# Macaron block on one core: four heads' scores on one wait, and features of the second feed-forward's first three groups made during attention

## The chip, the cores and the metric

The kernel runs on one NeuronCore of a Trainium2 chip. Five engines run their own streams of instructions and meet only at semaphores: PE (TensorE, matrix products into PSUM), ACT (ScalarE, exp, GELU and copies), DVE (VectorE, elementwise work, sums, 32x32 transposes), POOL (GpSimd) and SP (issues the DMAs). PSUM has eight banks of 128 x 512 float32. The metric is the device time of one execution in microseconds (us), the median of the runs.

## The reference, cut to what matters

```python
# x: 2 x 1024 x 128 float32; 8 heads of 8; 8 experts of 128 -> 256 -> 128; all inputs float32
def ffn(x):                                 # x already layer-normed, no affine part
    logits = x @ gate_w.T + gate_b          # 8 experts
    logits = logits * rsqrt(mean(logits**2) + eps) * rms_w
    g, idx = top_1(softmax(logits / 0.5))
    norm_g = masked(g) / (masked(g) + 1e-6)
    h = gelu(einsum('nd,edh->neh', x, w1) + b1)     # every expert, every token
    y = einsum('neh,ehd->ned', h, w2) + b2
    return (y * norm_g[:, None, None]).sum(axis=1)
def attn(x):
    q, k, v = heads((layernorm(x) * ln_w + ln_b) @ w_qkv)
    q, k = l2norm(q), l2norm(k)
    return merge(softmax(causal(8.0 * q @ k.T)) @ v) @ w_out
x = x + 0.5 * ffn(layernorm(x))
x = x + attn(layernorm(x))               # attn normalises once more
x = x + 0.5 * ffn(layernorm(x))
```

(`masked` keeps the gate of the chosen expert.)

## The kernel before, in words

The 2048 tokens are four groups of 512. Everything lives in SBUF between the first load and the last store. There are three stages: the first feed-forward (about 119 us), attention (about 119 to 188 us) and the second feed-forward (186 to 287 us).

**Feed-forward.** The eight experts' 2048 hidden units are 16 chunks of 128. For each group and chunk, PE makes three products up (`up`, L455 on) and three down (`down`, L479 on): float32 operands are held as a rounded part (`_hi`) and a remainder (`_lo`), so one product is hi*hi + hi*lo + lo*hi, each 128 x 512. ACT applies GELU from PSUM, DVE makes the remainder `h_lo`, and a ring of four PSUM banks and four SBUF slots keeps them apart. A group also needs its features: layer statistics and normalisation on DVE (`stats`, `aggregate`, `normalise`), a reciprocal root on POOL (`ln_once`), four transposes on PE (`ln_transpose`, L431), two copies on ACT (`ffn_features`, L727: the features `xf`, and their rounded part `xT_hi`), and the remainder `xT_lo` on POOL (`low_features`, L348). In each feed-forward the features of group g+1 are made while group g runs, at the chunks that `AT` names. In the second feed-forward only those of group 0 are made earlier, in attention.

**Attention.** Heads are packed four at a time (a "quad") with the operands of each head on its own 32 rows of the PE array. The list `steps` holds 80 half steps s; step k is the two half steps 2k and 2k+1, that is, four heads of one quad over one tile of 128 keys and up to 512 queries (`item`). A half step's scores (`scores`, L592 on) fill two PSUM banks, a set. There are three sets (`S_SETS`), six banks. ACT takes the exp of a whole set in one instruction (`exp_scores`, L797), 1024 elements a partition, or 512 where the last item of a causal block has half the queries; it writes `probs`. POOL masks the diagonal. PE then makes probabilities times values (`pv`, L606) three steps later (`PV_LAG`). PE's order in step k is: scores 2k, scores 2k+1, `pv(k-3)`, and at some steps a job. Before half step s is written, PE waits for the exp that read its set, s-3 (`set_reader`). So scores 2k wait for exp 2k-3, and scores 2k+1 for exp 2k-2.

**Jobs.** The list `jobs` (L242) is side work put between the products: PE's `fill(n)` (L631) writes one PSUM bank, DVE's `empty(n)` (L1137) takes it away, and every fill waits until the job before is emptied. A job with step number j is filled right after `pv(j)`, in PE's loop at k = j+3. With q1, q2, q3 = 6, 20, 26, the jobs are the last group's q, k and v; the output projections `project` of each pair of quads, which need `output` on DVE (L1118: a transpose of the accumulated output, reciprocal, scaling, transpose); and `ffn_ln` (L1159), the transposes of the normalised group 0 for the second feed-forward, at q3+5 = 31. All DVE work of attention stands in one list in the order of the jobs (L1196 on).

Of the kernel before, what the change touches and what calls it, by code (L numbers as in the profile page):

```python
# [30 lines left out]
P = 128  # L31
# [3 lines left out]
GROUP_TILES = 4  # L35
# [63 lines left out]
def build(nc, x, ln_w, ln_b, w_qkv, w_out, gate_w, gate_b, rms_w, w1, b1, w2, b2, out):  # L99
# [9 lines left out]
    with ctx:  # L109
# [118 lines left out]
        for st in steps:  # L228
# [16 lines left out]
                (q2 + 4, "project", (1, 0)), (q2 + 5, "project", (1, 1)),  # L245
                (q3 + 1, "project", (2, 0)), (q3 + 2, "project", (2, 1)), (q3 + 5, "ffn_ln", 0),
# [22 lines left out]

        def v_part(quad):  # L270
            return slice(SPREAD * quad, SPREAD * quad + HEAD_DIM)
# [13 lines left out]
        def ffn_groups(eng, layer, group):  # L285


            group(0)
            if layer == 0:
                for g in range(1, GROUPS - 1):  # L290
                    group(g)
            else:
                with eng.Fori(1, GROUPS - 1) as g:
                    group(g)
            group(GROUPS - 1)


# [50 lines left out]
        def low_features(eng, g):  # L348
            part = ds(g * GROUP, GROUP)
            eng.tensor_tensor(xT_lo[:, part], xf[:, FFN, :], xT_hi[:, part].bitcast(f32), ALU.subtract).then_inc(xT_ready, 1)  # L350
# [79 lines left out]
        def _(pe):  # L430
# [16 lines left out]
            def gate_product(F):  # L447
                pe.wait_ge(xf_done[FFN], F + 1)
                pe.wait_ge(gate_logits_done, F)
                for i in range(GROUP_TILES):  # L450
                    m = pe.matmul(ps[:, BANK_GATE, EXPERTS * i:EXPERTS * i + EXPERTS], xf[:, FFN, P * i:P * i + P],  # L451
                                  cols[:, COL_GATE:COL_GATE + EXPERTS], start=True, stop=True)
                m.then_inc(gate_mm, 1)

            def up(layer, F, c, g):  # L455
# [8 lines left out]
                if c == 0:  # L464
                    if layer == 1 and isinstance(g, int) and g == 0:
                        pe.wait_ge(xT_ready, F + 1)
                    else:
                        pe.wait_ge(hi_done, F + 1 - layer)
# [39 lines left out]
            def ffn_group(layer, g):  # L508
# [5 lines left out]
                for c in range(CHUNKS):  # L514
# [28 lines left out]
                    if c == at["ln_transpose"] and not last:  # L543
# [61 lines left out]

            def pv(k):  # L606
# [24 lines left out]
            def fill(n):  # L631
# [11 lines left out]
                elif kind in ("ln", "ffn_ln"):  # L643
                    norm = ATT if kind == "ln" else FFN
                    pe.wait_ge(xn_done[norm], GROUP_TILES * (LAST + 1 if kind == "ln" else GROUPS + 1))
# [39 lines left out]
            for k in range(quad_steps + PV_LAG):  # L685
                if k < quad_steps:
                    st = steps[2 * k]
                    if st["first"]:
                        p = Q_GROUPS * st["b"] + st["qg"]
                        if p < GROUPS // 2:  # L690
                            pe.wait_ge(kT_done, p + 1)
                        else:
                            pe.wait_ge(job_emptied, job_number["k_stack", p] + 1)
                    for s in (2 * k, 2 * k + 1):
                        if s < 4:
                            continue
                        if s == 4:
                            pe.wait_ge(qkv_copied, LAST)
                            pe.wait_ge(y_evac, GROUPS)
                            pe.wait_ge(xf_done[FFN], GROUPS)  # L700
                        scores(s)
                    if k == 0:
                        y_transposes(LAST, BANK_YT_LAST)
# [22 lines left out]
        def _(act):  # L726
            def ffn_features(layer, F, g):  # L727

                act.wait_ge(ln_t[FFN], F + 1 - layer)
# [86 lines left out]
            def ffn_group(layer, g):  # L816
# [5 lines left out]
                for c in range(CHUNKS):  # L822
# [24 lines left out]
                    if c == at["ln_copy"] and not last:  # L847
                        ffn_features(layer, F + 1, g + 1)
# [34 lines left out]
        def _(dve):  # L883
# [16 lines left out]
            def normalise(kind, n, g, tiles=range(GROUP_TILES), jobs_before=0):  # L900
                dve.wait_ge(rstd_done[kind], n + 1)
                dve.wait_ge(ln_t[kind], n - jobs_before)
# [126 lines left out]
            def ffn_group(layer, g):  # L1029
# [5 lines left out]
                for c in range(CHUNKS):  # L1035
                    if c == at["ln_aggregate"] and not last:
                        wait_stats(FFN, F + 1)
# [6 lines left out]
                    if not last:  # L1044
# [8 lines left out]
                        for half in range(2):  # L1053
                            if c == at["ln_normalise"][half]:
                                normalise(FFN, F + 1, g + 1, halves[half], jobs_before=layer)
# [42 lines left out]
            def first_stats(F):  # L1098
                stats(FFN, 0, range(GROUP_TILES))
# [37 lines left out]
            def empty(n):  # L1137
# [21 lines left out]
                elif kind == "ffn_ln":  # L1159
                    dve.wait_ge(gate_mm, GROUPS)  # L1160
                    dve.tensor_copy(xf[:, FFN, :], bank).then_inc(xf_done[FFN], 1)
                    dve.wait_ge(xf_done[FFN], GROUPS + 1)
                    dve.tensor_copy(xT_hi[:, 0:GROUP], bank).then_inc(job_emptied, 1)
# [65 lines left out]
        def _(pool):  # L1229
# [29 lines left out]
            def ffn_group(layer, g):  # L1259
# [4 lines left out]
                if not last:  # L1264
# [10 lines left out]
                if not last:  # L1275
                    pool.wait_ge(hi_done, F + 2 - layer)
                    low_features(pool, g + 1)
# [27 lines left out]
            for s, st in enumerate(steps):  # L1305
# [32 lines left out]
```

## Time and profile before

| what | before |
|---|---|
| median of three runs | 288.72 us (288.59 to 377.08) |
| profiled execution | 288.67 us, span on the core 286.9 us |
| PE busy | 274.2 us (96%) |
| ACT busy | 222.8 us (78%) |
| DVE busy | 216.9 us (76%) |
| POOL busy | 87.6 us (31%) |

The profiled execution stands 0.05 us under the median. Its 288.67 us are 1.8 us more than the span of the instructions on the core; that rest lies around the span. Busy shares are averages over three stages. In forty slices of the span ACT is at 9 tenths or more from the 17th to the 26th, which is attention, and PE is at 9 in nearly every slice from attention to the end. A recorded PE duration contains the pipeline, so starts are compared with starts.

### The profile page before, as it was taken

The numbers are of one execution on the slowest core, as the hardware profiler recorded it, in microseconds if no ns is written. First come the engines' busy times: TensorE is split into PE (matmuls) and PEld (weight loads), VectorE is DVE, ScalarE is ACT, GpSimd is POOL, SyncE is SP. The second block draws the span as 40 slices with busy tenths as digits, with TensorE's granted clock in tenths as the row PEclk, the third lists the DMA queues.
The fourth block names the chain that finished last, engine by engine and source line by source line (L and its number), as shares of the span: only waits on it lengthen the run. The fifth ranks groups of instructions, "written<-read, shape, count | busy, mean of one in ns | idle before, by whom it ended". The sixth has DMA issues, their size and how long they took to land.

```text
span 286.9 us, 5191 instructions
## 1 busy us (share of the span) xinstructions
PE 274.2 (96%) x1651; PEld 191.6 (67%) x1651; DVE 216.9 (76%) x573; ACT 222.8 (78%) x346; POOL 87.6 (31%) x155
## 2 busy tenths in 40 slices
PE   8998999999989998899998999999999999999994
PEld 8675788788778886432433432378888888888882
DVE  7699989888989889855588153078788898797765
ACT  2766876868787785999999999976785877677672
POOL 6326203301890383361438321401300310310010
PEclk9999999999999999999999999999999999999999
DMA  5720000000000000000000000000001000100101
GB/s 156 233 73 1 0 1 2 0 0 1 2 1 0 3 1 0 0 2 2 0 3 0 3 0 2 0 2 0 0 2 39 0 0 0 37 0 2 38 0 37
DMA packets 8107, 4.64 MB, mean 16 GB/s; under 512 B 690, under 2 KB 8084, under 8 KB 8084
## 3 DMA queue, kind: packets, MB, share of 16 engines
q1 hardware_dynamic: 8084, 4.35, 5.3%
q8 instruction: 12, 0.20, 0.3%
q14 instruction: 11, 0.09, 0.1%
HBM read 3.30 MB, written 1.05 MB: 15 GB/s over the span
## 4 chain that ended last, share of the span: by engine, by line
PE 73%; POOL 8%; ACT 8%; issue 5%; DVE 4%; DVEq 0%; POOLq 0%; ACTq 0%
PE ps L494 9%; PE ps L489 9%; PE ps L471 8%; PE ps L477 8%; PE ps L474 8%; PE ps L492 8%; PE ps L625 8%; ACT probs L803 5%; PE ps L602 3%; PE ps L664 2%; PE ps L656 2%; PE ps L451 2%; PE ps L580 2%; PE ps L442 2%; POOL rstd L1231 1%
## 5 line engine op out<-in xcount | busy, mean ns | idle before, releaser
L790 ACT ACTIVATE h<-ps,cols 128x512 f32<-128x512 f32 x128 | 87.9, 691 | 48.8 <-PE ps L477 43.5
L958 DVE TENSOR_TENSOR h_lo<-h,h_hi 128x512 fp32r<-128x512 f32 x128 | 92.0, 724 | 29.6 <-ACT h_hi L793 27.1
L803 ACT ACTIVATE probs<-ps 128x1024 f32<-128x1024 f32 (+1 forms) x80 | 67.0, 1013 | 0.6 <-PE ps L602 0.4
L489 PE MATMUL ps<-h_hi,w_hi 128*128 128x512 f32 x128 | 52.9, 413 | 0.3 <-DVE h_hi L956 0.3
L494 PE MATMUL ps<-h_lo,w_hi 128*128 128x512 f32 x128 | 50.9, 398 | 1.4 <-DVE h_lo L958 1.4
L471 PE MATMUL ps<-xT_hi,w_hi 128*128 128x512 f32 (+1 forms) x128 | 50.7, 396 | 0.1
L477 PE MATMUL ps<-xT_lo,w_hi 128*128 128x512 f32 (+1 forms) x128 | 50.0, 391 | 0.0
L492 PE MATMUL ps<-h_hi,w_lo 128*128 128x512 f32 x128 | 50.0, 391 | 0.0
L474 PE MATMUL ps<-xT_hi,w_lo 128*128 128x512 f32 (+1 forms) x128 | 49.9, 389 | 0.0
L793 ACT ACTIVATE h_hi<-ps,cols 128x512 fp32r<-128x512 f32 x72 | 49.2, 683 | 0.0
L1312 POOL TENSOR_SCALAR_AFFINE_SELECT probs<-probs 128x256 f32<-128x256 f32 x64 | 26.0, 431 | 46.5 <-ACT probs L803 46.0
L625 PE MATMUL ps<-probs,v_ones 128*32 128x512 f32 (+3 forms) x384 | 38.8, 495 | 0.0
L494 PEld LDWEIGHTS ps<-h_lo,w_hi 128*128 128x128 f32 x128 | 24.0, 188 | 9.5 <-DVE h_lo L958 4.4
L956 DVE CAST h_hi<-h 128x512 fp32r<-128x512 f32 x56 | 24.9, 444 | 7.0 <-ACT h L790 6.2
L489 PEld LDWEIGHTS ps<-h_hi,w_hi 128*128 128x128 f32 x128 | 24.1, 188 | 5.8 <-DVE h_hi L956 1.6
L471 PEld LDWEIGHTS ps<-xT_hi,w_hi 128*128 128x128 f32 x128 | 24.0, 188 | 5.6 <-ACT h L790 0.4
L477 PEld LDWEIGHTS ps<-xT_lo,w_hi 128*128 128x128 f32 x128 | 24.0, 188 | 5.5 <-DVE xT_lo L1182 0.2
L474 PEld LDWEIGHTS ps<-xT_hi,w_lo 128*128 128x128 f32 x128 | 24.0, 188 | 5.1
L492 PEld LDWEIGHTS ps<-h_hi,w_lo 128*128 128x128 f32 x128 | 24.1, 189 | 3.9
L602 PE MATMUL ps<-qT,kT 32*128 32x512 f16 (+3 forms) x192 | 21.3, 329 | 2.9 <-ACT probs L803 2.3
L602 PEld LDWEIGHTS ps<-qT,kT 32*128 32x128 f16 x192 | 6.5, 91 | 25.2 <-ACT probs L803 15.1
L1231 POOL TENSOR_TENSOR gate_rms<-gate_ms,neg_half 128x4 f32<-128x4 f32 x8 | 10.6, 1320 | 28.5 <-DVE gate_ms L923 28.5
(130 smaller groups left out, 288.4 us busy)
## 6 DMA issues: line engine op xcount, KB each, us to landing
w_raw<-in_L_ffn_w SPq DMA_DIRECT2D x8, 256.0 KB, 4.9
x_sb<-in_L_attn_x SPq DMA_DIRECT2D x3, 256.0 KB, 6.8
out_x<-x_sb SPq DMA_DIRECT2D x3, 256.0 KB, 2.3
x_sb<-in_L_attn_x SPq DMA_DIRECT2D x2, 128.0 KB, 2.2
out_x<-x_sb SPq DMA_DIRECT2D x2, 128.0 KB, 1.8
wout_sb<-in_L_attn_w_out SPq DMA_DIRECT2D x8, 4.0 KB
wqkv_sb<-in_L_attn_w_qkv SPq DMA_DIRECT2D x1, 96.0 KB, 6.0
small<-in_L_ffn_b SPq DMA_DIRECT2D x1, 8.0 KB
```

The source lines that it names most:

```text
L471: pe.matmul(bank, w1_hi[:, w], xT_hi[:, cols_g], start=True, stop=False)
L474: pe.matmul(bank, w1_lo[:, w], xT_hi[:, cols_g], start=False, stop=False)
L477: pe.matmul(bank, w1_hi[:, w], xT_lo[:, cols_g], start=False, stop=True).then_inc(up_done, 1)
L489: pe.matmul(y, w2_hi[:, w], h_hi[:, c % RING, :], start=(c == 0), stop=False)
L492: pe.matmul(y, w2_lo[:, w], h_hi[:, c % RING, :], start=False, stop=False)
L494: pe.matmul(y, w2_hi[:, w], h_lo[:, c % RING, :], start=False, stop=(c == CHUNKS - 1)).then_inc(down_done, 1)
L602: m = pe.matmul(ps[:, 2 * score_set(s) + hd, at:at + width], kT[rows, st["quad"], k0:k0 + P], qT[rows, st["quad"], qc:qc + width], start=T ...
L625: m = pe.matmul(ps[ROW * j:ROW * j + ROW, bank, q0:q0 + width], v_ones[:, SEQ // P * st["b"] + kt, 4 * st["quad"] + j, :], probs[:, (s + j ...
L790: first = nc.scalar.activation(h[:, slot, :], ps[:, BANK_H + slot, :], ACT.Gelu, bias=bias)
L793: nc.scalar.activation(h_hi[:, slot, :], ps[:, BANK_H + slot, :], ACT.Gelu, bias=bias).then_inc(gelu_done, 1)
L803: nc.scalar.activation(probs[:, s % P_SLOTS, :, 0:width], ps[:, bank:bank + 2, 0:width], ACT.Exp, scale=SCALE).then_inc(exp_done, 1)
L958: dve.tensor_tensor(h_lo[:, slot, :], h[:, slot, :], h_hi[:, slot, :].bitcast(f32), ALU.subtract).then_inc(split_done, 1)
```

## The change

Two things are changed.

1. In attention, from step 2 on, the two `scores` calls of a step become one `joint_scores`: one wait, for the exp that read the later of the two sets (exp 2k-2), and then the items in turn with the four heads innermost. Sets, banks and the two signals to ACT stay.
2. The features of groups 1 and 2 of the second feed-forward become jobs, like those of group 0. `ffn_ln` 0 moves from job step q3+5 to q2+3, `ffn_ln` 1 stands at q3+5, `ffn_ln` 2 at q3+9. Their statistics and normalisations are put into DVE's list, the two roots on POOL behind the masks of units 5 and 6. The features of groups 1 and 2 lie in `w_raw`, whose weights are no longer needed. In the second feed-forward only group 3's features are left to make (`turns`), and the hardware loop over its two middle groups is written out.

```diff
-                (q2 + 4, "project", (1, 0)), (q2 + 5, "project", (1, 1)),
-                (q3 + 1, "project", (2, 0)), (q3 + 2, "project", (2, 1)), (q3 + 5, "ffn_ln", 0),
+                (q2 + 3, "ffn_ln", 0), (q2 + 4, "project", (1, 0)), (q2 + 5, "project", (1, 1)),
+                (q3 + 1, "project", (2, 0)), (q3 + 2, "project", (2, 1)), (q3 + 5, "ffn_ln", 1),
+                (q3 + 9, "ffn_ln", 2),
...
+        def turns(layer, g):
+
+            return g < LAST if layer == 0 else g == LAST - 1
...
-                with eng.Fori(1, GROUPS - 1) as g:
-                    group(g)
-            group(GROUPS - 1)
-
+            for g in range(GROUPS):
+                group(g)
...
+            def joint_scores(k):
+
+                sets = 2 * k, 2 * k + 1
+                if set_reader(sets[1]) is not None:
+                    pe.wait_ge(exp_done, set_reader(sets[1]) + 1)
+                st = steps[sets[0]]
+                for n, (kt, q0, width, at) in enumerate(st["item"]):
+                    k0 = SEQ * st["b"] + P * kt
+                    qc = SEQ * st["b"] + GROUP * st["qg"] + q0
+                    for j in range(4):
+                        rows = slice(ROW * j, ROW * j + ROW)
+                        m = pe.matmul(ps[:, 2 * score_set(sets[j // 2]) + j % 2, at:at + width], kT[rows, st["quad"], k0:k0 + P],
+                                      qT[rows, st["quad"], qc:qc + width], start=True, stop=True)
+                        if n == len(st["item"]) - 1 and j % 2 == 1:
+                            m.then_inc(scores_done, 1)
...
-                if kind == "ffn_ln":
-                    normalise(FFN, GROUPS, 0)
                 empty(n)
...
+                if (kind, arg) == ("k_stack", LAST):
+                    normalise(FFN, GROUPS, 0)
+                if (kind, arg) == ("project", (1, 1)):
+                    dve.wait_ge(job_emptied, n + 1)
+                    first_stats(GROUPS + 1)
+                if (kind, arg) == ("project", (2, 1)):
+                    normalise(FFN, GROUPS + 1, 1)
+                    dve.wait_ge(job_emptied, n + 1)
+                    first_stats(GROUPS + 2)
                 if kind == "ffn_ln":
                     dve.wait_ge(job_emptied, n + 1)
-                    low_features(dve, 0)
+                    dve.wait_ge(xf_done[FFN], GROUPS + arg + 1)
+                    low_features(dve, GROUPS + arg, arg)
+                if (kind, arg) == ("ffn_ln", 1):
+                    normalise(FFN, GROUPS + 2, 2)
...
+                if s == 2 * last_quad[5] + 1:
+                    ln_once(GROUPS + 1)
+                if s == 2 * last_quad[6] + 1:
+                    ln_once(GROUPS + 2)
```

On PE, at steps 26 and 27 (scores, probabilities times values, the job), before:

```order
L602 MATMUL ps<-qT,kT 128x512 [waits exp_done,job_emptied]
L602 MATMUL ps<-qT,kT 128x512
L602 MATMUL ps<-qT,kT 128x512 [waits exp_done]
L602 MATMUL ps<-qT,kT 128x512
L625 MATMUL ps<-probs,v_ones 32x512 [waits mask_done]
L625 MATMUL ps<-probs,v_ones 32x512 x3
L602 MATMUL ps<-qT,kT 128x512 [waits exp_done]
L602 MATMUL ps<-qT,kT 128x512
L602 MATMUL ps<-qT,kT 128x512 [waits exp_done]
L602 MATMUL ps<-qT,kT 128x512
```

and in the changed kernel, whose lines are numbered some 24 higher (L626 is `joint_scores`, L672 the transposes of `ffn_ln`, L681 `project`):

```order
L626 MATMUL ps<-qT,kT 128x512 [waits exp_done,job_emptied]
L626 MATMUL ps<-qT,kT 128x512 x3
L650 MATMUL ps<-probs,v_ones 32x512 [waits mask_done]
L650 MATMUL ps<-probs,v_ones 32x512 x3
L672 MATMUL ps<-ident,xn 128x128 [waits xn_done_ffn,job_emptied]
L672 MATMUL ps<-ident,xn 128x128 x3
L626 MATMUL ps<-qT,kT 128x512 [waits exp_done]
L626 MATMUL ps<-qT,kT 128x512 x3
L650 MATMUL ps<-probs,v_ones 32x384 [waits mask_done]
L650 MATMUL ps<-probs,v_ones 32x384 x3
L650 MATMUL ps<-probs,v_ones 32x128 x4
L681 MATMUL ps<-wout_sb,o_feat 128x128 [waits o_ready,job_emptied]
```

The two waits on `exp_done` in a step are one, and four transposes stand between step 26 and step 27; the projection behind step 27 now waits for this job to be emptied.

On DVE, from the last k stack to the second projection's transposes, before:

```order
L1146 COPY kT<-ps 128x2x512 [waits job_filled]
L1170 TENSOR_TENSOR x_sb<-ps,x_sb 128x256 [waits job_filled] x2
L1121 STREAM_TRANSPOSE o_blocks<-ps 128x512 [waits pv_done]
L1124 RECIPROCAL rden<-o_blocks 128x32 [waits o_copied]
L1128 TENSOR_TENSOR o_scaled<-o_blocks,rden 128x32x8 [waits rden_done]
L1135 STREAM_TRANSPOSE o_feat<-o_scaled 128x512 [waits job_filled,o_scaled_done]
```

and in the changed kernel:

```order
L1169 COPY kT<-ps 128x2x512 [waits job_filled]
L927 TENSOR_SCALAR xn<-x_sb,mean_var,rstd 128x128 [waits ln_t_ffn,rstd_done_ffn]
L927 TENSOR_SCALAR xn<-x_sb,mean_var,rstd 128x128 x3
L1184 COPY xf<-ps 128x512 [waits gate_mm,job_filled]
L1185 CAST xT_hi<-ps 128x512
L359 TENSOR_TENSOR xT_lo<-xf,xT_hi 128x512 [waits xf_done_ffn,job_emptied]
L1192 TENSOR_TENSOR x_sb<-ps,x_sb 128x256 [waits job_filled] x2
L912 BN_STATS bn_part<-x_sb 128x6 [waits job_emptied]
L912 BN_STATS bn_part<-x_sb 128x6 x3
L921 BN_AGGR mean_var<-bn_part 128x2 [waits rstd_done_ffn,bn_done_ffn]
L921 BN_AGGR mean_var<-bn_part 128x2 x3
L1144 STREAM_TRANSPOSE o_blocks<-ps 128x512 [waits pv_done]
```

Four normalisations and three copies of group 0 have moved ahead of the two projections' additions, and the statistics of group 1 stand between those additions and the transposes (L1144 on) that the next projection needs.

## Rows read from the trace of the kernel before

**Rows 1.** One line's instructions: exp (L803), window 119 to 190 us.
```profile
L803 ACT ACTIVATE probs<-ps x78: 591/1060/1243, 119.1 to 184.1; 128x1024 f32<-128x1024 f32 x62, 128x512 f32<-128x512 f32 x16
```
**Rows 2.** Windows: start:end length, busy us (x instructions) of each engine, PE clock, DMA.
```profile
186.00:282.00 96.00, 96.00 (x455) 78.30 (x455) 77.23 (x193) 69.84 (x114) 13.11 (x13) 1.00 0.03 9
```
**Rows 3.** Timeline, ACT, exps 51, 52, 54, 56: start us, length us.
```profile
160.02 0.67 ACT L803 ACTIVATE probs<-ps 128x512 f32<-128x512 f32 x1
...
160.50 1.10 ACT L803 ACTIVATE probs<-ps 128x1024 f32<-128x1024 f32 x1
...
162.31 1.13 ACT L803 ACTIVATE probs<-ps 128x1024 f32<-128x1024 f32 x1
...
164.12 1.16 ACT L803 ACTIVATE probs<-ps 128x1024 f32<-128x1024 f32 x1
```
**Rows 4.** Timeline at step 17: PE's four score products, and the exp they release.
```profile
145.69 0.40 PE L602 MATMUL ps<-qT,kT 32*128 32x512 f16 x4
...
146.13 1.05 ACT L803 ACTIVATE probs<-ps 128x1024 f32<-128x1024 f32 x1
```
**Rows 5.** Timeline at step 3: the wait for exp 4, then exp 6.
```profile
121.62 0.09 PEld L602 LDWEIGHTS ps<-qT,kT 32*128 32x128 f16 x2 [0.30 <-ACT probs L803]
...
121.91 1.06 ACT L803 ACTIVATE probs<-ps 128x1024 f32<-128x1024 f32 x1
```
**Rows 6.** Timeline, PE, steps 26 to 34: L602 scores, L656 project, L647 ffn_ln.
```profile
160.25 0.39 PE L602 MATMUL ps<-qT,kT 32*128 32x512 f16 x2
...
162.98 0.71 PE L656 MATMUL ps<-wout_sb,o_feat 128*128 128x128 f32 x4
163.62 0.39 PE L602 MATMUL ps<-qT,kT 32*128 32x512 f16 x4
...
164.51 0.71 PE L656 MATMUL ps<-wout_sb,o_feat 128*128 128x128 f32 x4
...
168.47 0.71 PE L656 MATMUL ps<-wout_sb,o_feat 128*128 128x128 f32 x4
169.12 0.40 PE L602 MATMUL ps<-qT,kT 32*128 32x384 f16 x8
...
170.44 0.71 PE L656 MATMUL ps<-wout_sb,o_feat 128*128 128x128 f32 x4
...
175.13 0.65 PE L647 MATMUL ps<-ident,xn 128*128 128x128 f32 x4
```
**Rows 7.** Timeline, DVE, the pieces that the change moves or puts between.
```profile
139.59 0.86 DVE L889 BATCH_NORM_STATS2 bn_part<-x_sb 128x6 f32<-128x128 f32 x4
140.48 0.38 DVE L898 BATCH_NORM_AGGREGATE mean_var<-bn_part 128x2 f32<-128x6 f32 x4
...
158.99 0.69 DVE L1146 COPY kT<-ps 128x1024 f16<-128x1024 f16 x1 [1.13 <-PE ps L580]
...
165.60 0.71 DVE L1121 STREAM_TRANSPOSE o_blocks<-ps 128x512 f32<-128x512 f32 x1
...
167.19 0.71 DVE L1135 STREAM_TRANSPOSE o_feat<-o_scaled 128x512 f32<-128x512 f32 x1
...
171.54 1.42 DVE L904 TENSOR_SCALAR xn<-x_sb,mean_var,rstd 128x128 f32<-128x128 f32 x4
175.83 0.69 DVE L1161 COPY xf<-ps 128x512 f32<-128x512 f32 x1 [2.87 <-PE ps L647]
...
177.28 0.69 DVE L350 TENSOR_TENSOR xT_lo<-xf,xT_hi 128x512 fp32r<-128x512 f32 x1
```
**Rows 8.** Timeline, PE, second feed-forward: around a group's four transposes, and without them.
```profile
228.01 0.39 PE L477 MATMUL ps<-xT_lo,w_hi 128*128 x1
...
229.01 0.40 PE L492 MATMUL ps<-h_hi,w_lo 128*128 128x512 f32 x1
...
200.67 0.39 PE L477 MATMUL ps<-xT_lo,w_hi 128*128 128x512 f32 x1
...
201.12 0.39 PE L492 MATMUL ps<-h_hi,w_lo 128*128 128x512 f32 x1
```

More of the change, by code:

```diff
@@ L268, in pair_of_job, with features, ln_groups_turned @@
             return steps[2 * min(jobs[n][0], quad_steps - 1)]["unit"] // QUADS
+        def features(F):
+            if F in (GROUPS + 1, GROUPS + 2):
+                return w_raw[:, GROUP * (F - GROUPS - 1):GROUP * (F - GROUPS)]
+            return xf[:, FFN, :]
+        def ln_groups_turned(n):
+            return n if n < GROUPS else GROUPS
         def v_part(quad):
@@ L464, in up @@
                 if c == 0:
-                    if layer == 1 and isinstance(g, int) and g == 0:
+                    if layer == 1 and g < LAST:
                         pe.wait_ge(xT_ready, F + 1)
                     else:
-                        pe.wait_ge(hi_done, F + 1 - layer)
+                        pe.wait_ge(hi_done, F + 1 - LAST * layer)
                 if starts:
@@ L542, in ffn_group @@
                         scores(0)
-                    if c == at["ln_transpose"] and not last:
+                    if c == at["ln_transpose"] and turns(layer, g):
                         if layer or not first:
@@ L693, in _ @@
                             pe.wait_ge(job_emptied, job_number["k_stack", p] + 1)
[L694 to L701, printed above, removed]
+                    if k == 2:
+                        pe.wait_ge(qkv_copied, LAST)
+                        pe.wait_ge(y_evac, GROUPS)
+                        pe.wait_ge(xf_done[FFN], GROUPS)
+                    if k >= 2:
+                        joint_scores(k)
                     if k == 0:
@@ L846, in ffn_group @@
                         affine_features(g - 1)
-                    if c == at["ln_copy"] and not last:
+                    if c == at["ln_copy"] and turns(layer, g):
                         ffn_features(layer, F + 1, g + 1)
@@ L898, in aggregate, with normalise @@
                     dve.bn_aggr(mean_var[:, kind, i, :], bn_part[:, kind, i, :]).then_inc(mv_done[kind], 1)
[L900 removed]
+            def normalise(kind, n, g, tiles=range(GROUP_TILES)):
                 dve.wait_ge(rstd_done[kind], n + 1)
[L902 removed]
+                dve.wait_ge(ln_t[kind], ln_groups_turned(n))
                 for i in tiles:
@@ L1035, in ffn_group @@
                 for c in range(CHUNKS):
-                    if c == at["ln_aggregate"] and not last:
+                    if c == at["ln_aggregate"] and turns(layer, g):
                         wait_stats(FFN, F + 1)
@@ L1043, in ffn_group @@
                         weight_parts(2 + c // 5)
-                    if not last:
+                    if turns(layer, g):
                         if c == at["ln_stats"][0]:
@@ L1054, in ffn_group @@
                             if c == at["ln_normalise"][half]:
-                                normalise(FFN, F + 1, g + 1, halves[half], jobs_before=layer)
+                                normalise(FFN, F + 1, g + 1, halves[half])
                     for half in range(2):
@@ L1098, in first_stats @@
             def first_stats(F):
-                stats(FFN, 0, range(GROUP_TILES))
+                stats(FFN, F - GROUPS, range(GROUP_TILES))
                 wait_stats(FFN, F)
@@ L1263, in ffn_group @@
                     inverse_lengths(pool, g - 2, range(2))
-                if not last:
+                if turns(layer, g):
                     ln_once(F + 1)
@@ L1274, in ffn_group @@
                     low_parts(pool, g - 2)
-                if not last:
-                    pool.wait_ge(hi_done, F + 2 - layer)
-                    low_features(pool, g + 1)
+                if turns(layer, g):
+                    pool.wait_ge(hi_done, F + 2 - LAST * layer)
+                    low_features(pool, F + 1, g + 1)
             pool.memset(ones[:, :], 1.0).then_inc(const_self, 1)
```

20 lines of the change are left out of this document (7 added, 13 removed).

## The prediction

> **What bounds the kernel now.** The windows came first: from 186 to 282 us PE is busy for all 96.00 us, at full granted clock, while DVE and ACT each have idle time [rows 2]. So the second feed-forward costs what PE's instructions there cost. Then the exp line: 78 exps start between 119.1 and 184.1 us, 62 of 1024 elements and 16 of 512 [rows 1]. Single exps show the cadence: a narrow one is followed after 0.48 us (160.02 to 160.50), a wide one after 0.905 (two from 160.50 to 162.31, 1.81) [rows 3]. The last exp is narrow, so the 77 intervals need 62 x 0.905 + 15 x 0.48 = 63.3 us, and they take 65.0. Attention is bound by ACT's exps, and only 1.7 us of it are exps that waited. The sum is therefore: PE instructions taken from the second feed-forward, minus what the change does to the start of exps.
>
> One more constant is needed. At step 17 all four score products start at 145.69 and the exp at 146.13: 0.44 us from PE's start to the exp [rows 4].
>
> **Saved in the second feed-forward.** Two groups lose their four transposes on PE. From the product before them to the second product behind them it is 1.00 us (228.01 to 229.01), for two product starts that otherwise take 0.45 (200.67 to 201.12) [rows 8]. That is 0.55 us a group and 1.1 us for two. The ACT copies, DVE statistics and POOL roots of these groups were hidden under PE, which never idled [rows 2], and give nothing. Nor does the written-out loop, for the same reason: no PE idle stands at its ends. Bounds of this part: 1.0 to 1.2.
>
> **The joint wait.** Scores 2k used to be free once exp 2k-3 was done; they now wait for exp 2k-2. PE is released 0.19 us after the start of exp 2k-1 at step 3 (exp 5 starts one narrow exp, 0.48, before 121.91) and 0.23 at step 26 (160.02 to 160.25) [rows 3, 5, 6]. With 0.44 more, exp 2k can start 0.63 to 0.67 us after exp 2k-1. If exp 2k-1 is wide it is due after 0.905, and 0.23 us are to spare: no cost. If it is narrow it is due after 0.48, and the exp is 0.15 to 0.19 late: 121.62 + 0.44 = 122.06 instead of 121.91 at step 3, 160.69 instead of 160.50 at step 26. Seven steps follow a narrow one (3, 6, 13, 20, 23, 26, 33). I count 3 and 6, 0.35 us together; 26 is in the chain below, and the others I put down as covered by PE already being behind. Bounds: nothing, and 7 x 0.19 = 1.3. Products and probabilities times values (pv) themselves are neither more nor fewer. PE does not gain: it had to wait for exp 2k-2 before pv anyway.
>
> At step 17 the four products start together, so packing by four is already there when the banks are free [rows 4]. The Trainium skill, TensorEngine Tiling (Array Packing), Theoretical Speedup, gives up to 4x for a small dimension of at most 32. By the Trainium skill the joint issue would turn two half-filled passes into one; by the row it finds one pass already where PE is late, and elsewhere the first pair filled waiting time.
>
> **The moved and added jobs.** Each `ffn_ln` job is four transposes on PE (about 0.6 us; the record says 0.65), two copies on DVE that must end before the next job is filled (1.45 us from 175.83 to 177.28), then a remainder of 0.7, and 1.42 of normalisation ahead [rows 6, 7]. PE needs 1.32 us for scores and a wide pv (169.12 to 170.44) [rows 6], of the 1.81 that two exps allow [rows 3]: 0.49 to spare, less than a fill. At the old place (step 34) such a job was already standing. The new place at step 26 is followed at once by two projections. Worked forward in us, in the clock of the old trace:
> - Step 26: PE starts at 160.25, is at the fill at 161.57. The normalisation of group 0 now follows the k stack's copy and is ready, 158.99 + 0.69 + 1.42 = 161.10 [rows 7]. Transposes until 162.17.
> - Step 27: exp 54 at 162.17 + 0.44 = 162.61, was 162.31 [rows 3]. PE is at the projection at 163.49 but the job is emptied only at 161.57 + 0.70 + 1.45 = 163.72 (0.70 is 175.13 to 175.83 [rows 6, 7]). Projection, 0.64 (162.98 to 163.62) [rows 6], until about 164.4.
> - Step 28: exp 56 at 164.83, was 164.12: 0.7 us lost so far. The second projection is filled at 164.4 + 0.89 (163.62 to 164.51) = 165.3.
> - DVE then had its addition and began `output` 1.09 us after that fill (164.51 to 165.60) [rows 6, 7]; now 166.4. But group 1's statistics stand in front, 1.27 us (139.59 to 140.48, + 0.38), and `output` takes 2.30 (165.60 to 167.19, + 0.71) [rows 7]: done at 169.95.
> - Step 30: PE would be at the projection of pair 2 at about 169.1 and waits 0.9 us, to 170.0. It was filled at 168.47. Step 31 starts at 170.65 instead of 169.12 [rows 6], and exp 62 is late by the same 1.5 us.
>
> After that the list has room. `ffn_ln` 1 stands at the old step. Its normalisation begins after the second projection's addition, around 173.2, and is ready near 174.7; PE comes to it after 175.13 + 1.5 = 176.6. `ffn_ln` 2 at step 38 costs PE 0.6 shortly before the exps end, after which PE has three pv to do before it can start the feed-forward; between 0 and 0.6, I take 0.3. The roots on POOL wait for the statistics, and behind them stand the masks of unit 6; pv needs those three steps, 5.4 us, later, so this is hidden, and would cost only what it exceeds that.
>
> Sum for attention: 0.35 + 1.5 + 0.3 = 2.15 later. Together with the 1.1 saved: 288.67 + 2.15 - 1.1 = 289.7 us, against the profiled execution of 288.67 (the median is 288.72, 0.05 more).
>
> **Rivals.**
> - *The fills are absorbed.* If exps keep their starts (the statistics shorter, PE ahead of its exps at step 26), only the saving is left: 288.67 - 1.1 = 287.6. For it: ACT lost only 1.7 us with eleven jobs before step 31. Against: PE and DVE rows at steps 26 to 30 add up past the slack of 0.49. It ends on the other side, faster than before, and decides as soon as attention loses less than the 1.1 us saved: `output` done by 169.0 in the clock above would be enough. Chance 0.17.
> - *Joint issue frees PE.* Were four heads' products quicker than two and two wherever PE is late, all late exps could go: 288.67 - 1.7 - 1.1 = 285.9. The start at one time in [rows 4] speaks against it. Chance 0.03.
> - *Nothing has slack.* The joint wait costs 0.19 at all seven steps (1.3), the chain 1.5, and both other fills 0.6 each: 4.0 - 1.1 = 2.9, or 291.6. For it: PE is close to full in attention. Against: steps 35 to 39 have no other job. Chance 0.09.
> - *The wait is late at every step.* If the four products took 0.3 us longer behind a fresh wait than at step 17, the 31 steps from step 2 on that follow a wide exp would lose 0.07 each beyond the 0.23 spare (2.2 us), and the seven behind a narrow one 0.49 each (3.4). With the chain (1.5), the last fill (0.3) and the saving that is 288.67 + 7.4 - 1.1 = 295.0. It decides from 0.23 us of delay on. Nothing in the rows speaks for it: the first pair starts the same way before. Chance 0.02.
>
> **Numbers.** Forecast as summed, own range 288.4 to 291.0: 0.69. The range 288.0 to 291.2 leaves out most of the first rival, the second, and the upper two. A difference of 2%, 5.8 us, is about what a measurement of this kernel can tell from no change. Only the last rival reaches it upward (294.5), and none reaches 282.9. With a little for what I do not see: faster 0.01, same 0.96, slower 0.03.
>
> **What would show it.** In the changed profile: exp intervals of about 0.65 instead of 0.48 behind narrow exps at steps 3 and 6; exp 62 later than exp 52 by 1.3 us or more than before; a PE wait for `o_feat` of about 0.9 at step 30; PE product starts 0.227 apart across the old loop and no L442 in groups 0 and 1; the second feed-forward 1.1 us shorter. I am wrong if the last exp starts less than 1.1 us later than before, if PE waits appear in the second feed-forward, or if the exps after wide ones come more than 0.905 apart at steps that have no job.

## The result and the profile after

The changed kernel takes 290.23 us, the median of nine runs (289.6 to 291.42), beside 288.87 us for the kernel before in nine runs. The ratio is 1.0051, with a 95% interval of 1.0038 to 1.0065: 1.5 us slower, between 1.1 and 1.9. The profiled execution stands at 289.6 us, span 287.9. Within 2% this is no difference; with the interval it is a small loss. One of the nine executions before was slow (377.08 us) and is left out of the ratio.

The line of the exps in the changed kernel (count, length in ns, first and last start):

```profile
L826 ACT ACTIVATE probs<-ps x78: 591/1024/1142, 118.7 to 185.8; 128x1024 f32<-128x1024 f32 x62, 128x512 f32<-128x512 f32 x16
```

It answers to [rows 1]. The same 78 exps now take 67.06 us from first to last start, where they took 64.93: attention is 2.13 us longer. A window of the changed kernel (columns as in [rows 2]) shows the second feed-forward bound by PE as before, busy for 95.00 of 95.00 us:

```profile
188.00:283.00 95.00, 95.00 (x448) 77.36 (x447) 72.06 (x169) 67.72 (x109) 8.11 (x7) 1.00 0.03 9
```

Its length is read from the first product up to the first transpose behind the last product:

```profile
187.71 0.50 PE L480 MATMUL ps<-xT_hi,w_hi 128*128 128x512 f32 x1
...
284.03 0.44 PE L744 MATMUL ps<-ident,yT 128*128 128x128 f32 x2 [0.57 <-ACT yT L836]
```

That is 96.32 us. Before it was 97.19:

```profile
185.91 0.50 PE L471 MATMUL ps<-xT_hi,w_hi 128*128 128x512 f32 x1
...
283.10 0.44 PE L721 MATMUL ps<-ident,yT 128*128 128x128 f32 x2 [0.56 <-ACT yT L813]
```

So 0.87 us are saved there. Between the start of the last exp and the first product up lie 1.91 us instead of 1.83. Together 2.13 + 0.08 - 0.87 = 1.34 us, which is what the medians show. (In this one execution the stages before exp 2 were 0.41 us shorter, so its span differs by 0.9 only. The change does not touch them, and executions differ there: over the thirteen kept traces exp 2 starts between 118.56 and 119.40 us.)

Where the 2.13 us arise is seen on PE in steps 26 to 31, timeline of the changed kernel:

```profile
160.50 0.40 PE L626 MATMUL ps<-qT,kT 32*128 32x512 f16 x4 [0.59 <-ACT probs L826]
160.82 1.07 PE L650 MATMUL ps<-probs,v_ones 128*32 128x512 f32 x8
161.82 0.65 PE L672 MATMUL ps<-ident,xn 128*128 128x128 f32 x4
162.41 0.39 PE L626 MATMUL ps<-qT,kT 32*128 32x512 f16 x4
162.73 1.07 PE L650 MATMUL ps<-probs,v_ones 128*32 128x384 f32 x16
163.86 0.71 PE L681 MATMUL ps<-wout_sb,o_feat 128*128 128x128 f32 x4
164.50 0.39 PE L626 MATMUL ps<-qT,kT 32*128 32x512 f16 x4
...
168.17 1.06 PE L650 MATMUL ps<-probs,v_ones 128*32 128x512 f32 x8
170.23 0.68 PE L681 MATMUL ps<-wout_sb,o_feat 128*128 128x128 f32 x4 [1.00 <-DVE o_feat L1158]
170.84 0.40 PE L626 MATMUL ps<-qT,kT 32*128 32x384 f16 x8
```

Scores, pv, the new fill at 161.82, and at once the next scores; then, in the projection at 170.23, the wait of 1.00 us for `o_feat`. This projection was filled at 168.47 before [rows 6]. DVE at the same time:

```profile
166.15 0.42 DVE L1192 TENSOR_TENSOR x_sb<-ps,x_sb 128x256 f32<-128x256 f32 x1 [1.11 <-PE ps L681]
166.60 0.87 DVE L912 BATCH_NORM_STATS2 bn_part<-x_sb 128x6 f32<-128x128 f32 x4
167.51 0.38 DVE L921 BATCH_NORM_AGGREGATE mean_var<-bn_part 128x2 f32<-128x6 f32 x4
167.81 0.68 DVE L1144 STREAM_TRANSPOSE o_blocks<-ps 128x512 f32<-128x512 f32 x1
...
169.37 0.71 DVE L1158 STREAM_TRANSPOSE o_feat<-o_scaled 128x512 f32<-128x512 f32 x1
```

Group 1's statistics, 166.60 to 167.81, stand between the addition and the output's transposes, which PE waits for.

### The profile page after: what moved, and what is told of

The parts are those of the page before. It is cut to its first block, busy times and chain, and to the rows that moved or that the text cites. A ratio compares the mean times of both kernels' runs of the same rounds, so it can differ in the third digit from the quotient of the medians.

```text
span 287.9 us, 4963 instructions
## 1 busy us (share of the span) xinstructions
PE 269.4 (94%) x1651; PEld 189.0 (66%) x1651; DVE 220.9 (77%) x579; ACT 221.6 (77%) x342; POOL 85.2 (30%) x153
## 4 chain that ended last, share of the span: by engine, by line
PE 68%; ACT 8%; POOL 8%; issue 6%; DVE 6%; SPq 1%; DMA 1%; DVEq 0%; ACTq 0%; POOLq 0%
PE ps L503 9%; PE ps L498 9%; PE ps L480 8%; PE ps L486 8%; PE ps L483 8%; PE ps L501 8%; ACT probs L826 6%; PE ps L650 5%; PE ps L626 2%; PE ps L681 2%; PE ps L460 2%; POOL rstd L1263 1%; PE ps L579 1%; PE ps L589 1%; DVE h_lo L981 1%
## 5 line engine op out<-in xcount | busy, mean ns | idle before, releaser
L826 ACT ACTIVATE probs<-ps 128x1024 f32<-128x1024 f32 (+1 forms) x80 | 67.9, 965 | 1.9 <-PE ps L626 1.3
L480 PE MATMUL ps<-xT_hi,w_hi 128*128 128x512 f32 x128 | 50.6, 396 | 0.3 <-ACT xT_hi L886 0.3
L486 PE MATMUL ps<-xT_lo,w_hi 128*128 128x512 f32 x128 | 50.0, 391 | 0.0
L483 PE MATMUL ps<-xT_hi,w_lo 128*128 128x512 f32 x128 | 49.9, 390 | 0.0
L979 DVE CAST h_hi<-h 128x512 fp32r<-128x512 f32 x56 | 24.3, 435 | 8.1 <-ACT h L813 6.8
L626 PE MATMUL ps<-qT,kT 32*128 32x512 f16 (+3 forms) x180 | 14.2, 330 | 7.3 <-ACT probs L826 6.5
L626 PEld LDWEIGHTS ps<-qT,kT 32*128 32x128 f16 x180 | 4.1, 91 | 24.4 <-ACT probs L826 15.7
```

Source lines behind the costliest of these rows:

```text
L480: pe.matmul(bank, w1_hi[:, w], xT_hi[:, cols_g], start=True, stop=False)
L483: pe.matmul(bank, w1_lo[:, w], xT_hi[:, cols_g], start=False, stop=False)
L486: pe.matmul(bank, w1_hi[:, w], xT_lo[:, cols_g], start=False, stop=True).then_inc(up_done, 1)
L826: nc.scalar.activation(probs[:, s % P_SLOTS, :, 0:width], ps[:, bank:bank + 2, 0:width], ACT.Exp, scale=SCALE).then_inc(exp_done, 1)
```

## The experiments

The runs were compared with runs of the kernel before on the same chip. For each profiled execution the exps' starts were set against those of the kernel before, both counted from exp 2. "Attention" is the time from the start of exp 2 to that of exp 79, "FFN 2" the second feed-forward, read as above.

| kernel | median us | before us | ratio (95%) | attention | FFN 2 |
|---|---|---|---|---|---|
| before | | | | 64.93 | 97.19 |
| changed | 290.23 | 288.87 | 1.0051 (1.0038 to 1.0065) | 67.06 | 96.32 |
| x0 changed again | 290.29 | 288.87 | 1.0058 (1.0044 to 1.0072) | 67.07 | 96.25 |
| x1 joint only | 289.58 | 288.91 | 1.0021 (1.0013 to 1.0030) | 65.71 | 97.21 |
| x2 jobs only | 289.44 | 288.91 | 1.0022 (1.0010 to 1.0035) | 66.39 | 96.27 |
| x3 statistics behind | 289.05 | 288.91 | 1.0000 (0.9988 to 1.0012) | 66.61 (a) | 96.25 |
| x4 early slot | 288.19 | 288.91 | 0.9975 (0.9966 to 0.9983) | 65.09 | 96.27 |
| x6 gate later | 287.61 | 288.87 | 0.9961 (0.9949 to 0.9974) | 65.10 | 95.89 |
| x10 the same again | 288.00 | 288.96 | 0.9954 (0.9936 to 0.9972) | 66.01 (a) | 95.87 |
| x9 with joint | 287.95 | 288.96 | 0.9960 (0.9945 to 0.9975) | 65.68 (a) | 95.93 |
| x7 loop only | 289.26 | 288.87 | 1.0011 (1.0002 to 1.0021) | 65.48 (a) | 97.28 |
| x11 the same again | 289.28 | 288.91 | 1.0017 (1.0004 to 1.0030) | 64.92 | 97.27 |
| x8 joint behind wide | 288.55 | 288.87 | 0.9991 (0.9981 to 1.0001) | 65.78 (a) | 97.24 |

(a) These profiled executions hold an event at steps 4 and 5 of 0.4 to 0.95 us that belongs to no kernel; it is shown in the last section, and left out of the next table.

How much later than before the first exp of each step came, less the same for the step ahead of it, in us (only steps where one kernel has more than 0.04):

| step | changed | x1 joint | x2 jobs | x3 | x4 |
|---|---|---|---|---|---|
| 3 | 0.23 | 0.23 | 0 | 0.22 | 0 |
| 6 | 0.25 | 0.25 | 0 | 0.22 | 0 |
| 11 | -0.11 | -0.11 | 0.02 | -0.11 | 0.02 |
| 20 | 0.22 | 0.22 | 0 | 0.22 | 0 |
| 22 | -0.24 | -0.23 | 0 | -0.24 | 0 |
| 23 | 0.20 | 0.20 | 0 | 0.20 | 0 |
| 26 | 0.25 | 0.25 | 0 | 0.25 | 0.26 |
| 27 | 0.11 | 0.02 | 0.28 | 0.11 | 0.02 |
| 28 | 0.28 | 0 | 0.28 | 0.28 | 0 |
| 31 | 0.89 | -0.01 | 0.90 | -0.01 | -0.01 |
| 32 | -0.01 | -0.06 | 0 | -0.06 | -0.06 |
| 33 | 0 | -0.02 | 0 | -0.06 | -0.02 |

### One part alone: the joint wait, the jobs

x1 is the kernel before with this in place of the two calls of `scores` (`joint_scores` itself is that of the change):

```diff
-                    for s in (2 * k, 2 * k + 1):
-                        if s < 4:
-                            continue
...
-                        scores(s)
+                    if k == 2:
+                        pe.wait_ge(qkv_copied, LAST)
...
+                    if k >= 2:
+                        joint_scores(k)
```

> The kernel before with the joint scores alone; jobs, features and the hardware loop stay as before. Theory (the wait costs only behind narrow exps, and is given back where PE or DVE is behind anyway): exp 2k comes about 0.2 us late at steps 3, 6, 20, 23 and 26, part of it is absorbed at steps 11 and 22, the last exp starts about 0.5 us later, and the time is 0.5 us over the kernel before (0.3 to 0.8). Rival one (the joint wait is free, PE was behind anyway): no difference, under 0.1 us. Rival two (packing by four frees PE): faster, by up to the 1.7 us that exps waited.

Measured: 1.0021, 0.6 us slower, and attention 0.78 longer. The wait costs 0.20 to 0.25 us at exactly the five steps named, and at no step behind a wide exp. Of the seven steps behind a narrow one, 13 and 33 cost nothing, and 20 was given back at 22, where PE waits for DVE's `k_stack` in any case (0.81 us before, 0.62 here). Both rivals fall: it is neither free nor a gain. Step 3 in its timeline, the release of the four products and then exp 6:

```profile
121.96 0.40 PE L617 MATMUL ps<-qT,kT 32*128 32x512 f16 x4 [1.11 <-ACT probs L817]
...
122.39 1.02 ACT L817 ACTIVATE probs<-ps 128x1024 f32<-128x1024 f32 x1
```

The exp starts 0.43 us behind the products, as in [rows 4].

x2 is the opposite: the changed kernel with the old loop over `scores(s)`, the same diff with its signs turned round.

> The changed kernel with the two separate waits of the kernel before; jobs and features stay changed. Theory (both parts cost, independently): exps late by 0.1 to 0.3 us at step 27, 0.3 at 28 and about 0.9 at 31, last exp 1.3 to 1.5 us later than before, second feed-forward 0.9 shorter, so 0.5 to 0.8 us over the kernel before and 0.6 to 0.9 under the changed one. Rival (the stalls at steps 27 to 31 come from the joint wait, or absorb it): then either this is 0.9 under the kernel before, or equal to the changed one.

Measured: 1.0022, 0.6 us slower; attention 1.46 longer, 0.28, 0.28 and 0.90 us at steps 27, 28 and 31; FFN 2 0.92 shorter. The parts cost independently: 0.78 + 1.46 = 2.24, where the changed kernel shows 2.13. Together they lose 0.17 less at step 27 (0.11 where the jobs alone lose 0.28): the exps already lost 0.25 at step 26, and that covers part of PE's lateness. Against that, x1 gains 0.06 at step 32, and the changed kernel does not.

### Undoing one cause: statistics behind the output

```diff
                     output(pair_of_job(n) - 1)
+                if (kind, arg) == ("project", (2, 0)):
+                    dve.wait_ge(job_emptied, n)
+                    first_stats(GROUPS + 1)
                 empty(n)
...
-                if (kind, arg) == ("project", (1, 1)):
-                    dve.wait_ge(job_emptied, n + 1)
-                    first_stats(GROUPS + 1)
```

> The changed kernel with one move on DVE: the statistics of group 1 come after the transposes, reciprocal and scaling of pair 2's output instead of ahead of them. Theory (they delay the operand of the next projection): PE no longer waits 0.9 us at step 30, exp 62 comes 0.9 us earlier, time 0.8 to 0.9 us under the changed kernel. Rival (PE is behind by itself there, because of the job at step 26): nothing gained, within 0.2 us of the changed kernel.

Measured: ratio 1.0000 to the kernel before; the changed kernel has 1.0058 (x0), so about 1.7 us less by the ratios and 1.2 by the medians. The trace shows 0.90 of it at step 31, and 0.05 and 0.06 more at the two steps behind it. DVE and PE there:

```profile
168.57 0.71 DVE L1158 STREAM_TRANSPOSE o_feat<-o_scaled 128x512 f32<-128x512 f32 x1
...
169.21 0.83 DVE L912 BATCH_NORM_STATS2 bn_part<-x_sb 128x6 f32<-128x128 f32 x4
169.66 0.71 PE L681 MATMUL ps<-wout_sb,o_feat 128*128 128x128 f32 x4
```

`o_feat` is finished before PE comes to it, the statistics fill DVE's idle time after it, and nothing waits for them. The rival, that PE was late by itself, falls. The expectation was 0.8 to 0.9. The medians' 1.2 is near the 1.0 of the traces; what more there is stays open, since x0 and x3 ran on different chips and a larger share of x0's executions have the half clock of the last section (4 of 6, against 5 of 12).

### Another slot for the first job

x4 has the separate waits of the kernel before and the move of x3, and puts group 0's job one step earlier:

```diff
-                (q2 + 3, "ffn_ln", 0), (q2 + 4, "project", (1, 0)),
+                (q2 + 2, "ffn_ln", 0), (q2 + 4, "project", (1, 0)),
```

with `normalise(FFN, GROUPS, 0)` ahead of the k stack's copy.

> Separate waits as before, the statistics of group 1 behind the output as in the run before this one, and group 0's features filled one step earlier (loop step 25, behind a pv of half width), with its normalisation ahead of the k stack's copy. Theory (a fill is free where the pv beside it is narrow and no projection follows in the next step): attention as long as before within 0.3 us, and the 0.9 us of the second feed-forward kept: 0.6 to 1.0 us under the kernel before. Rival (PE has no room for three more fills anywhere): 0.6 us or more of attention lost, time equal to the kernel before or above.

Measured: 0.9975, 0.7 us faster than before. The 0.28 and 0.28 us at steps 27 and 28 are gone; 0.26 at step 26 came in their place. PE in x4:

```profile
158.64 0.64 PE L650 MATMUL ps<-probs,v_ones 128*32 128x256 f32 x8
159.28 0.66 PE L672 MATMUL ps<-ident,xn 128*128 128x128 f32 x4
159.86 0.40 PE L611 MATMUL ps<-qT,kT 32*128 32x512 f16 x4
```

The narrow pv takes 0.64 us, the fill 0.58, and the scores of step 26 come at 159.86. Their exp is due early, since exps 50 and 51 are narrow. So the rival (no room anywhere) falls, and the theory held in size but for the place: the fill is not free, it costs 0.26 instead of 0.56. That the narrow exps are the reason was not tested by itself.

### The gap in the second feed-forward

The changed kernel saves 0.87 us there, not 1.1. From a group's first product to the next group's, the first three groups take 25.25, 23.79 and 23.79 us before and 24.61, 23.21 and 24.13 in the changed kernel: 0.64 and 0.58 are saved in the first two, and 0.34 are lost in the third. Its trace has PE starts 0.39 and 0.34 us apart in the third group, where most are 0.23, and its weight loads wait for DVE:

```profile
257.20 0.19 PEld L498 LDWEIGHTS ps<-h_hi,w_hi 128*128 128x128 f32 x1 [0.23 <-DVE h_hi L979]
...
257.23 0.47 PE L498 MATMUL ps<-h_hi,w_hi 128*128 128x512 f32 x1
...
257.54 0.40 PE L501 MATMUL ps<-h_hi,w_lo 128*128 128x512 f32 x1
257.93 0.19 PEld L503 LDWEIGHTS ps<-h_lo,w_hi 128*128 128x128 f32 x1 [0.43 <-DVE h_lo L981]
257.93 0.50 PE L503 MATMUL ps<-h_lo,w_hi 128*128 128x512 f32 x1
...
258.27 0.39 PE L480 MATMUL ps<-xT_hi,w_hi 128*128 128x512 f32 x1
```

Two and a half microseconds earlier a gate operation of 32 elements takes 1.25 us on DVE, as long as POOL works on `xT_lo`:

```profile
254.70 1.29 POOL L359 TENSOR_TENSOR xT_lo<-xf,xT_hi 128x512 fp32r<-128x512 f32 x1 [4.50 <-ACT xT_hi L757]
```

```profile
254.57 0.18 DVE L951 TENSOR_TENSOR gate_tmp<-logits,gate_rms 128x32 f32<-128x32 f32 x1
254.79 1.25 DVE L953 TENSOR_TENSOR logits<-gate_tmp,rms_w_row 128x32 f32<-128x32 f32 x1
```

The Trainium skill, SBUF — State Buffer, section SBUF: two separate sides, says that a DVE operation with two SBUF inputs and a GpSimd operation that reads SBUF take one shared port pair for a whole instruction each, and that the later one is blocked until the other ends. The trace agrees: 254.79 + 1.25 = 256.04, and POOL ends at 255.99. The kernel before has such a collision too, two small operations later in the list, and the operation that is held in the changed kernel takes 0.19 us there:

```profile
254.25 0.19 DVE L930 TENSOR_TENSOR logits<-gate_tmp,rms_w_row 128x32 f32<-128x32 f32 x1
...
254.69 1.03 DVE L934 TENSOR_TENSOR gate_tmp<-logits,gate_max 128x32 f32<-128x32 f32 x1
```

x6 is x4 with the gate operations of this group moved past POOL's subtraction:

```diff
+AT_SIXTH = dict(AT, gate_shift=11, gate_tanh=12, gate_weight=13)
...
-            return AT_ZERO if (layer, g) == (0, 0) else AT_LAST if (layer, g) == (0, LAST) else AT_THIRD if (layer, g) == (0, 2) else AT_FIRST if (layer, g) == (1, 0) else AT
+            return AT_ZERO if (layer, g) == (0, 0) else AT_LAST if (layer, g) == (0, LAST) else AT_THIRD if (layer, g) == (0, 2) else AT_FIRST if (layer, g) == (1, 0) else AT_SIXTH if (layer, g) == (1, LAST - 1) else AT
```

> The kernel with the earlier slot for group 0's features and the statistics behind the output, and one more move: in the third group of the second feed-forward the four small gate operations on DVE stand two chunks later (11 instead of 9), past POOL's 1.3 us subtraction that makes xT_lo. Theory (a small DVE operation that starts while POOL subtracts is held 1.25 us, and h_hi comes late for PE): the PE starts 0.39 and 0.34 us apart in that group become 0.227, and the time is 0.2 to 0.3 us under the kernel with the earlier slot, 1.0 us under the kernel before. Rival (the gap comes from the features' transposes or from ACT): the gap stays, no difference.

Measured: 0.9961. FFN 2 is 95.89, 0.38 under x4, and the gap is gone (the same four products start 0.23, 0.23 and 0.22 apart):

```profile
255.38 0.39 PE L499 MATMUL ps<-h_hi,w_hi 128*128 128x512 f32 x1
255.61 0.39 PE L502 MATMUL ps<-h_hi,w_lo 128*128 128x512 f32 x1
255.84 0.39 PE L504 MATMUL ps<-h_lo,w_hi 128*128 128x512 f32 x1
256.06 0.39 PE L481 MATMUL ps<-xT_hi,w_hi 128*128 128x512 f32 x1
```

The third group takes 23.77 us here. So the 1.1 us foreseen were there, 1.30 in fact, and the changed kernel gave 0.4 back in this collision. The rival, the transposes or ACT, falls: the transposes stand where they stood, and the waits of the changed kernel's weight loads are for DVE. x10 is x6 run again beside x9; it agrees (0.9954).

> The kernel of the gate run again, on the chip of the run before this one, to compare the two: 1.0 to 1.3 us under the kernel before, as first measured, by every theory.

### The loop, and the joint wait behind wide steps

x7 and x11 are the kernel before with the hardware loop written out and nothing else:

```diff
-            group(0)
...
-                with eng.Fori(1, GROUPS - 1) as g:
-                    group(g)
-            group(GROUPS - 1)
+            for g in range(GROUPS):
+                group(g)
```

> The kernel before with the hardware loop over the two middle groups of the second feed-forward written out, and nothing else. The prediction costed this at nothing. Theory from the trace of the changed kernel: in the loop POOL starts its subtraction about 0.2 us after the copy it waits for, written out 0.1 us, and this shift alone brings the DVE hold one small operation earlier; then groups 1 and 2 show a PE gap each and the time is 0.2 to 0.5 us over the kernel before. Rival (the loop costs nothing either way and the gap comes from the missing features work): no gap, within 0.1 us.

> The kernel before with the loop of the second feed-forward written out, again. The first time it was 0.3 us over the kernel before, and its profiled execution had PE's granted clock at half for 3.4 us at the start of attention, which some executions of every kernel show. Theory (the written-out loop costs nothing, the 0.3 us came from that clock): within 0.2 us of the kernel before, and attention as in the kernel before if the profiled execution keeps full clock. Rival (the written-out code costs 0.3 us by itself): 0.3 us again, with an attention or a feed-forward longer by that much at full clock.

Measured: 1.0011 and 1.0017, both intervals above 1, 0.3 to 0.5 us. In the traces FFN 2 is 0.08 to 0.09 us longer and at full clock (x11) attention is 64.92 against 64.93. Half of my theory for x7 held: with the loop written out, the held operation is the one that is held in the changed kernel, in both middle groups (230.71 and 254.53 in x7), and no longer the one two places behind it:

```profile
254.53 1.25 DVE L923 TENSOR_TENSOR logits<-gate_tmp,rms_w_row 128x32 f32<-128x32 f32 x1
```

The other half fell: PE feels it by 0.04 us a group (23.83 us instead of 23.79 for each), its starts at that place are at most 0.26 apart, and there is no gap of 0.3. So the written-out code alone sets which operation is held, and the 0.34 us that the changed kernel loses come only when the rest of the second part is there too. Which piece of it makes PE feel the hold was not tested.

What more the medians show lies outside the instructions. The time of an execution less the span of its instructions is 2.0 to 2.1 us in all 24 executions of x7 and x11, and 1.7 to 1.8 in every execution of each other kernel, the changed one and the kernel before included. The mean spans are as before within 0.1 us (287.12 beside 287.10, 287.21 beside 287.14). So my theory for x11, that the clock made the difference, falls, and so does its rival, that a stage is longer by 0.3 us. Why these 0.3 us stand around the span of this program stays open; as the changed kernel has its loop written out too and does not have them, they are no part of its time.

x8 leaves the joint wait away only behind narrow steps:

```diff
...
+                    narrow_before = k >= 1 and sum(w for _, _, w, _ in steps[2 * k - 2]["item"]) < GROUP
+                    if k >= 2 and narrow_before:
+                        scores(2 * k)
+                        scores(2 * k + 1)
+                    elif k >= 2:
+                        joint_scores(k)
```

> The kernel before with the joint scores at all steps but those that follow a narrow step, which keep two waits. Theory (the joint wait has 0.23 us to spare behind a wide exp and lacks 0.2 behind a narrow one): no exp is late, the time is that of the kernel before within 0.15 us. Rival (the joint wait costs at PE-late steps too, or joint issue saves something that the narrow steps hid): 0.3 us or more away from the kernel before, up or down.

Measured: 0.9991, and the interval holds 1: no difference shown, though the median is 0.3 us lower, more than the 0.15 expected. The costs at steps 3, 6, 20, 23 and 26 are all zero. x9 adds the same to x6:

> The kernel of the gate run with the joint scores added at all steps but those behind a narrow step. Theory (joint issue costs nothing behind wide steps, and gives 0.1 us at step 11, where both items of a diagonal pair are written and PE is late): 0.0 to 0.2 us under the same kernel without it. Rival (the joint issue saves more, as the 0.3 us under the kernel before could be read): 0.3 us or more under it.

Measured: 0.9960 beside 0.9954 for the same kernel without it. Joint issue, where it costs nothing, gains nothing that these runs can tell. The 0.1 us that the expectation puts down to it at step 11 is not its gain: x10 and x7, which have separate waits, gain 0.08 and 0.09 there behind their delay at step 4, as x1 does behind its own.

> The changed kernel once more, beside the runs of this call, so that they can be compared with it. Expected: 1.3 to 1.5 us over the kernel before, as measured first; second feed-forward with one PE gap of about 0.3 us in its third group, by every theory.

x0 measured 1.0058; the first measurement is confirmed, gap included.

## Why the prediction was right, and where its parts were off

The forecast was 289.7 us, 1.0 above the profiled execution; measured are 290.23, 1.4 above the median of before. It lies in the range, and the likeliest case was the right one.

- **What bounds.** Right. Attention is the exps and their waits; FFN 2 is PE. The sum of the two stages and the piece between them gives 1.34.
- **The chain at steps 26 to 31.** Right place by place. Foreseen: exp 54 late by 0.3, exp 56 by 0.7, exp 62 by 1.5, a wait for `o_feat` of 0.9. x2, which has the chain alone: 0.28, 0.56, 1.46; the wait is 1.00 us long. x3 takes the last 0.9 away; x4 has 0.26 in place of the 0.56 ahead of it. After step 31 nothing more was lost, as said; the `ffn_ln` 2 fill cost 0.08, not 0.3.
- **The joint wait.** The mechanism was right, behind narrow exps only, and the size was off. I counted 0.35 for it outside the chain; there it cost 0.59 (what the changed kernel's exps had lost by step 25), and by itself, step 26 included, 0.78 (x1). Two terms were mis-sized. Each late exp is 0.20 to 0.25, not 0.15 to 0.19, because the four products released by one wait start up to 0.30 behind the start of exp 2k-1 (at step 3 of x1 exp 5 starts at 122.39 - 0.23 - 0.48 = 121.68, the products at 121.96, 0.28 behind; the exp intervals at steps 3 and 6 of the changed kernel are 0.70 and 0.72, not 0.65), where I had read 0.19 to 0.23 off the pair. And "covered by PE already being behind" was right for 13 and 33, wrong for 23, and 20 was covered by the DVE wait at 22.
- **Saved in the second feed-forward.** Foreseen 1.1 (bounds 1.0 to 1.2), measured 0.87. The step that failed is "give nothing" for the work of the other engines: with that work gone and the loop written out, another small DVE operation fell under POOL's, and a collision that before fell where PE did not notice it cost about 0.4 (x6: 1.30 saved without it). The rule that a hidden engine cannot matter was too simple. The prediction had named PE waits in this stage as a sign of being wrong, and this sign came; the other two did not, beyond 0.02 us on the exp behind a late one.
- **The loop at nothing.** Nearly right for the stages: 0.08 in the trace, by the same collision. The 0.3 us around the span that x7 and x11 show are not in the changed kernel.
- **The errors balanced.** The joint wait ahead of the chain took 0.24 more than counted (0.59 for 0.35), the last fill 0.22 less (0.08 for 0.3), the chain was right (1.54 for 1.5). So 2.21 us were lost where 2.15 were forecast, and the first two errors cancel by luck. What is left of the difference is the saving, 0.23 short.
- **The rivals.** "The fills are absorbed" gave 287.6 (it counted eleven jobs before step 31; the list has twelve); x4 and x6 reach 288.2 and 287.6, but with the slot and the statistics moved, not as the change has it. "Joint issue frees PE" is refuted by x1, x8 and x9: what the Trainium skill, TensorEngine Tiling (Array Packing), Theoretical Speedup, gives for packing by four (up to 4x) is already had, since the four products start together when the banks are free [rows 4]. "Nothing has slack" and "late at every step" did not happen.

The best kernel found, x6, takes 287.61 us, 1.3 below the kernel before: jobs as in the change, separate waits, the first job one step earlier, the statistics behind the output, the gate operations out of POOL's way.

## What to carry to other kernels

Where one engine runs back to back, ask of each merged wait how much sooner the second of two signals was needed, and check it at the shortest instructions of that engine: here 0.905 us of exp hid the later release and 0.48 did not. Work that moves into an engine's slack must be placed in that engine's order behind whatever the bounding chain waits for next; 1.2 us of statistics placed ahead of a transpose cost 0.9, behind it nothing. And work taken off an engine that is not the bound can still cost, if it shifts that engine's small operations under a neighbour's long one.

## What the runs showed that was not expected

**Half clock for 3.4 us at the start of attention.** In five of the thirteen profiled executions of this study PE's granted clock falls to half, from 2.4 to 1.2 GHz, between 121.2 and 122.5 us, for 3.4 us. It is not a matter of the kernel: x6 and x10 are the same program. Windows of x10 and then of x6 (columns as in [rows 2], granted clock third from the right):

```profile
118.00:120.50 2.50, 1.55 (x14) 0.72 (x12) 1.99 (x8) 2.23 (x3) 0.92 (x3) 1.00 0.00 0
120.50:122.00 1.50, 1.06 (x8) 0.36 (x12) 1.43 (x7) 1.50 (x4) 1.35 (x5) 0.74 0.00 0
122.00:124.00 2.00, 2.00 (x12) 0.21 (x14) 1.79 (x11) 1.59 (x2) 1.83 (x4) 0.50 0.04 8
```

```profile
118.00:120.50 2.50, 1.58 (x14) 0.72 (x12) 1.97 (x8) 2.21 (x3) 0.91 (x3) 1.00 0.00 0
120.50:122.00 1.50, 1.04 (x8) 0.38 (x12) 1.43 (x8) 1.50 (x4) 1.35 (x5) 1.00 0.00 0
122.00:124.00 2.00, 2.00 (x32) 0.62 (x24) 1.79 (x11) 2.00 (x3) 1.83 (x4) 1.00 0.03 8
```

In these two microseconds x10 has 12 matmul records to x6's 32: the eight products of a pv (L651) that take 1.07 us in x6, from 121.67, take 1.94 in x10, from 121.86. Its exp 8 comes 0.95 us late; in the other four it is 0.4 to 0.9. Just before, from 118 to 120.5, PE was busy 1.55 of 2.50 us in x10 and 1.58 in x6, so that stretch does not tell them apart. The changed kernel's profile and that of the kernel before both had full clock there, so their comparison is untouched.

The mean clock of an execution tells which ones have it: 0.990 to 0.993 in the profiled executions with the stretch, 0.996 to 1.000 in those without. Of the 35 executions of the kernel before that were measured beside x1, 19 have 0.994 or less, with a mean time of 289.16 us, and 16 have more, with 288.59. Seven of the nine executions of the changed kernel have 0.994 or less. The loss is there at either clock: beside x0, on one chip, the means are 289.86 us for the changed kernel against 288.63 without the stretch (two executions and fifteen), and 290.47 against 289.08 with it (four and fourteen).

**DVE held by POOL for 1.25 us on an operation of 32 elements** (above), where the same operation takes 0.19 in the kernel before, when POOL's begins later.
